# A four-part sequence network with 32 experts: blocks shared ten to six between the two sets of expert tiles, and three gathers in flight beside the tiles

## What is computed

```python
x = x + _L0_attn_ref(_layernorm(x), ...)        # delta rule
x = x + _L0_ffn_ref(_layernorm(x), ...)         # 8 of 32 experts a token, plus a shared one
x = x + _L1_attn_ref(_layernorm(x), ...)        # h = dA_t * h + dBx_t, then y = hs @ C.T + D * x
x = x + _L1_ffn_ref(_layernorm(x), ...)         # quantized in blocks of 32, then @ weight.T
```

## Time and profile before

| | |
|---|---|
| median of 3 runs | 3666.69 us (3666.28 to 3671.66) |
| the profiled execution | 3663.13 us |
| its span | 3661.3 us |
| PE, DVE, ACT, POOL busy | 74%, 59%, 43%, 29% of the span |
| chain that ended last | DMA 55% (scatters 40%, gathers 14%), PE 28%, issue 7%, DVE 5% |
| granted TensorE clock, mean | 0.825 |

### The profile page before, as it was taken

The page is one execution under the profiler, slowest core; times in us unless marked ns, Lnnn a source line. Parts: engine busy times, 40 slices in busy tenths (PEclk is TensorE's granted clock), DMA queues, the critical chain, the costliest instruction groups (busy, mean ns, idle before and its releaser), DMA issues.

```text
span 3661.3 us, 109753 instructions
## 1 busy us (share of the span) xinstructions
PE 2712.2 (74%) x46188; PEld 2021.3 (55%) x46188; DVE 2153.5 (59%) x4702; ACT 1565.2 (43%) x2625; POOL 1048.7 (29%) x1028
## 2 busy tenths in 40 slices
PE   4578888888878887875207999997898888643544
PEld 2355555555555655554106888886777777422322
DVE  4878888888888888772201222213444444676675
ACT  4445555545544555511003444444555554432231
POOL 0001333333332333333330000014434431366661
PEclk8768788888888788766558999998999999876666
DMA  6001111111114111111317999997888887333331
GB/s 241 8 9 36 61 56 61 50 64 62 62 62 148 62 61 55 56 56 57 141 52 245 303 305 304 304 311 232 266 280 262 272 266 247 120 94 94 99 93 34
DMA packets 240349, 511.79 MB, mean 140 GB/s; under 512 B 38770, under 2 KB 63860, under 8 KB 239732
## 3 DMA queue, kind: packets, MB, share of 16 engines
q1 hardware_dynamic: 133396, 270.32, 22.6%
q0 software_dynamic: 49152, 134.28, 11.8%
q10 hardware_dynamic: 57312, 100.16, 7.5%
HBM read 303.82 MB, written 200.80 MB: 138 GB/s over the span
## 4 chain that ended last, share of the span: by engine, by line
DMA 55%; PE 28%; issue 7%; DVE 5%; ACT 3%; POOL 1%; SPq 0%; ACTq 0%; POOLq 0%; DVEq 0%
DMA scr_xs<-xn_r,idx 40%; DMA yg<-scr_ys,idx_y 14%; PE ps L629 13%; PE ps L637 6%; PE ps L618 3%; DVE tmp L1426 1%; DVE tu L1429 1%; PE ps L377 1%; DVE conv L1356 1%; PE ps L706 1%; PE ps L669 1%; DMA out<-x 1%; POOL yg L869 1%; PE ps L688 1%; PE ps L364 0%
## 5 line engine op out<-in xcount | busy, mean ns | idle before, releaser
L851 POOL DMA_INDIRECT scr_xs<-xn_r,idx x512 | 528.9, 1033 | 1407.5 <-DMA scr_xs<-xn_r,idx 1062.4
L869 POOL DMA_INDIRECT yg<-scr_ys,idx_y x512 | 519.7, 1015 | 1129.2 <-DMA scr_ys<-y 574.4
L1721 DVE TENSOR_TENSOR h<-sg,ps 128x256 f32<-128x256 f32 x318 | 133.1, 420 | 829.3 <-ACT sg L1106 790.6
L629 PE MATMUL ps<-xT,wr 128*128 128x256 f32 x2544 | 617.1, 386 | 0.0
L629 PEld LDWEIGHTS ps<-xT,wr 128*128 128x128 f32 x2544 | 470.5, 195 | 62.0 <-issue 8.6
L1748 DVE SCALAR_TENSOR_TENSOR x<-yg,wsel,x 128x256 f32<-128x256 f32 x512 | 247.8, 485 | 220.3 <-DMA yg<-scr_ys,idx_y 201.9
L637 PE MATMUL ps<-wr,h 128*128 128x256 f32 x1272 | 334.1, 386 | 57.8 <-DVE h L1721 31.5
L914 ACT ACTIVATE xT<-ps 128x512 f32<-128x512 f32 x382 | 225.3, 594 | 210.5 <-PE ps L618 173.2
L618 PE MATMUL ps<-identity,xt 128*128 128x128 f32 x1272 | 195.7, 277 | 149.9 <-DMA xt<-scr_xs 149.9
L637 PEld LDWEIGHTS ps<-wr,h 128*128 128x128 f32 x1272 | 242.9, 192 | 98.4 <-DVE h L1721 34.0
L914 ACT ACTIVATE y<-ps 128x512 f32<-128x512 f32 x318 | 189.8, 597 | 202.0 <-PE ps L637 186.8
(11 more groups left out here) (244 smaller groups left out, 4216.8 us busy)
## 6 DMA issues: line engine op xcount, KB each, us to landing
wr<-in_wexp SPq DMA_DIRECT2D x318, 384.0 KB
xt<-scr_xs SPq DMA_DIRECT2D x318, 256.0 KB
scr_ys<-y ACTq DMA_DIRECT2D x318, 256.0 KB
scr_xs<-zeros SPq DMA_DIRECT2D x128, 256.0 KB
x_in<-in_x SPq DMA_DIRECT2D x64, 128.0 KB
x_res<-in_x SPq DMA_DIRECT2D x64, 128.0 KB
scr_xs<-xn_r,idx POOLq DMA_INDIRECT x512, 2.6
scr_x<-x_res SPq DMA_DIRECT2D x16, 512.0 KB
```

The lines of the kernel that those rows point to most:

```text
L629: last = pe.matmul(ps[:, bank, half * TILE:(half + 1) * TILE], wr[:, t % NW, at:at + EI], xT2[:, t % NH, k, :], start=k == 0, stop=k == G - 1)
L851: nc.gpsimd.indirect_dma_start(xs[i // HB][:, :], bass.IndirectOffsetOnAxis(idx[:, i % 2, c, k:k + 1], 0), xn_r[:, i % 2, c, :], None).the ...
L869: nc.gpsimd.indirect_dma_start(yg[:, n % NG, k, :], None, ys[h][:, :], bass.IndirectOffsetOnAxis(idx_y[:, i, c, k:k + 1], 0))\
```

## The change

Blocks 0 to 9 belong to the first set of tiles and blocks 10 to 15 to the second. CAP becomes 4 * 10 * 128 + 256 = 5376 rows (4352 before). The sets have NTH = [191, 127] tiles; NT stays 318. The tiles that run alone are 191. SL = 13, and a helper `Share` hands out 13 slots in an iteration at the places where 22 were handed out, each in proportion. `slots(NT)` and the iterations without tiles begin at i == 8 and no longer at 6. `tables(0)` runs behind block 9 and `clear_ends(0)` in step 11, both two steps later. The gathers count on four semaphores in place of two, for each of which `combine` waits. For blocks 0 to 9 a gather waits for the third before it, for blocks 10 to 15 for the second as before.

```diff
+class Share:
+    def __init__(self, run, per, of):
+        self.run, self.per, self.of, self.at, self.done = run, per, of, 0, 0
+    def __call__(self, weight):
+        self.at += weight
+        want = self.at * self.per // self.of
+        self.run(want - self.done)
+        self.done = want
...
-    if "P" in on and (on["P"] + 1) % (NB // 2) == 0:
-        on["H"] = on["P"] // (NB // 2)
+    if "P" in on and on["P"] + 1 in (NB * 5 // 8, NB):
+        on["H"] = int(on["P"] + 1 == NB)
...
-    CAP = B * T // HALVES + TILE
-    NTH = B * T // HALVES * TOPK // TILE + E - 1
-    NT = HALVES * NTH
-    NQ = -(-NTH // P)
+    FIRST = (NB * 5 // 8, NB)
+    CAP = B * FIRST[0] * TB + TILE
+    NTH = [B * TB * blocks * TOPK // TILE + E - 1 for blocks in (FIRST[0], NB - FIRST[0])]
+    NT = sum(NTH)
+    NQ = -(-max(NTH) // P)
...
-        SL = -(-(NTH + LAG - 30) // (HB - 2))
+        SL = -(-(NTH[1] + LAG - 30) // (FIRST[0] - 2))
...
-        s_yg = [sem(f"s_yg{n}") for n in range(2)]
+        s_yg = [sem(f"s_yg{n}") for n in range(4)]
...
-                if i == HB - 2:
+                if i == FIRST[0] - 2:
                     slots(NT)
                     banks = tuple(range(8))
                 if i:
                     quant_turns(i - 1)
                 skips(i)
-                slots(2)
+                share(2)
                 outputs(i)
-                slots(1)
+                share(1)
                 if i:
                     quant_rows(i - 1, 0)
-                slots(2)
+                share(2)
                 if i:
                     quant_rows(i - 1, 1)
-                slots(5)
+                share(5)
                 if i + 1 < NB:
                     delta_turns(i + 1)
-                    slots(2)
+                    share(2)
                     deltas(i + 1)
-                    slots(1)
+                    share(1)
                     inputs(i + 1)
-                    slots(2)
+                    share(2)
                     means(i + 1)
-                slots(SL - 15)
+                share(7)
...
-                if j == HB + 1:
+                if j == FIRST[0] + 1:
                     clear_ends(0)
...
-                        if fetched >= 2:
-                            pool.wait_ge(s_yg[fetched % 2], 16 * (fetched // 2))
+                        landed = fetched - (3 if i < FIRST[0] else 2)
+                        if landed >= 0:
+                            pool.wait_ge(s_yg[landed % 4], 16 * (landed // 4 + 1))
...
-                for way in range(2):
-                    dve.wait_ge(s_yg[way], 16 * TOPK // 2 * (n + 1))
+                for way in range(4):
+                    dve.wait_ge(s_yg[way], 16 * TOPK // 4 * (n + 1))
```

More of the change, by code:

```diff
@@ L656, in _ @@
             turn_tile(1)
-            slots(NTH)
+            slots(NTH[0])
             def delta_turns(i):
@@ L729, in outputs @@
                     done(last, bank)
+            share = Share(slots, SL, 22)
             slots(23)
@@ L857, in _ @@
             for i in range(NB):
-                h = i // HB
-                if i % HB == 0:
+                h = int(i >= FIRST[0])
+                if i in (0, FIRST[0]):
                     for n in range(NY):
-                        pool.wait_ge(s_ys[n], 16 * (-(-(NTH * (h + 1) - n) // NY)))
+                        pool.wait_ge(s_ys[n], 16 * (-(-(sum(NTH[:h + 1]) - n) // NY)))
                 for c in range(NC):
@@ L1207, in _ @@
                     quant_turns(i - 1)
-                slots(6)
+                share(6)
                 root("quant", i)
@@ L1211, in _ @@
                     root("tail", i + 1)
-                slots(2)
+                share(2)
                 if i + 1 < NB:
                     tail_rows(i + 1)
-                slots(2)
+                share(2)
                 if i + 1 < NB:
                     delta_turns(i + 1)
-                    slots(2)
+                    share(2)
                     softplus(i + 1)
-                    slots(3)
+                    share(3)
                     decays(i + 1)
-                slots(SL - 15)
+                share(7)
                 if i:
@@ L1734, in _ @@
                 rows_of_y(p)
[L1735 to L1736 removed]
+                slots(NTH[0] // NB)
+            slots(NTH[0] % NB)
             def combine(i, c, k0=0, k1=TOPK):
                 n = NC * i + c
[L1740 to L1741 removed]
+                for way in range(4):
+                    dve.wait_ge(s_yg[way], 16 * TOPK // 4 * (n + 1))
                 if c == 0 and k0 == 0:
@@ L1753, in combine, with combine_between @@
                     last.then_inc(s_comb, 1)
-            def combine_between(i, c):
+            def combine_between(i, c, run=slots):
                 combine(i, c, 0, TOPK // 2)
-                slots(1)
+                run(1)
                 combine(i, c, TOPK // 2)
-                slots(1)
+                run(1)
             def tail_means(i):
@@ L1794, in quant_rows @@
                 sQ.did(normalize(xq, x3[:, i % NX3], "quant", i, sQ))
-                slots(1)
+                share(1)
                 sQ.wait(dve)
-                quantize(xq[:].rearrange("p c d -> p (c d)"), qb[:], qc[:], NC * D // QB, sQ, slots)\
+                quantize(xq[:].rearrange("p c d -> p (c d)"), qb[:], qc[:], NC * D // QB, sQ, share)\
                     .then_inc(s_xn["quant"], 1)
+            share = Share(slots, SL, 22)
             slots(9)
```

41 lines of the change are left out of this document (19 added, 22 removed).

## The result

The changed kernel takes 3759.0 us (3719.0 to 3784.3, 4 runs) and the kernel before, on the same chip, 3669.2: a ratio of **1.021 [1.013, 1.029]**. Ratios here compare means, and an execution over 1.5% above the fastest of its kernel, such as the one at 3784.3, is left out of them. The forecast was 3614, with 3655 as its upper end; the direction is wrong. The span of the profiled execution is 3761.2, 99.9 us more than before.

A forecast was written before the change was run, and what follows sets the result against it. The prediction took scatters, then PE on tiles, then gathers (tail, 55.1 us a block) as limits. 2533.7 + 147 + 66.0 + 6 x 74.0 + 12.8 + 328.9 + 76.5 = 3608.9, plus 5.4: 3614 us, range 3585 to 3655.

The forecast's parts named there:

- The third gather: Start of the shared stretch: with three in flight, gathers come every 1.8 us in place of 2.41.
- the lead-in: From the start of the shared stretch to `deltas(1)`: 147 us, 36.9 less than before.
- The tail: Second set's gathers: 192 in place of 256 at 1.722 us, 110 us less, then 76.5 as before.
- Iterations with tiles: Shared stretch: 13 slots in place of 22 take 27.2 us out of each; 66.0, then six of 74.0.
- cover term: Iterations with tiles: fewer slots between hand-overs add 2.0 us each, between 0 and 6.3, taken from PE's idle time.
- The first whole iteration: `deltas(1)` to `deltas(2)`, without the wait for `out`: 64.0 us plus 2.0 added, so 66.0.
- the third gather without effect: Rival, shared stretch: DMA sets 2.41 us a gather, 320 gathers in a row, 3724 us; chance 0.07.
- thin cover: Rival, iterations with tiles: hand-overs show in full, 6.3 us added and not 2.0, 3644 us; chance 0.13.
- PE idle over 17 us in an iteration: Sign in iterations with tiles that the forecast is wrong through cover; 13 us of idle time was forecast.
- CAP, tables, semaphores: Edits put at nothing: addresses change, two steps move; two more waits per combination, 0.5 us a block on DVE with slack.
- The 8 us allowed for the scatters: Before the first tile: scatters go one at a time as before, 8 us allowed either way.
- The locked port: Rival, gathers' issue: each as long as the longest, 1.97 us, a rate of 2.27, 3679 us; chance 0.02.

The follow-up runs named there:

- e2: Kernel before (eight to eight) with three gathers in flight for the first set only, chip 1: 0.990 of the kernel before.
- e1: Changed kernel with two gathers in flight throughout (ten to six), chip 1: 1.006 of the kernel before.
- a2: Changed kernel run again as it is, chip 5, no stops: 0.993 of the kernel before.
- e10: Changed kernel (ten to six) with three gathers in flight for all blocks, chip 15: 0.972 of the kernel before.
- e8: Kernel before (eight to eight) with three gathers in flight for all blocks, chip 5: 0.965 of the kernel before.
- a3: Changed kernel run again as it is, chip 15, no stops: 0.991 of the kernel before.
- a4: Changed kernel run again as it is, chip 7, with stops: 1.023 of the kernel before.
- e4: Kernel before with only the changed kernel's larger CAP, chip 1: 1.000 of the kernel before.
- e6: Kernel before (eight to eight) with four gathers in flight for the first set, chip 5: 0.988 of the kernel before.
- e1c: Changed kernel with two gathers in flight throughout (ten to six), chip 7, no stops: 1.005 of the kernel before.
- e8b: Kernel before (eight to eight) with three gathers in flight for all blocks, chip 7, with stops: 1.016 of the kernel before.

## Why the prediction was wrong

- **The third gather** did what was forecast: 1.76 us against 1.8. By itself it is worth 1203.8 - 1174.8 = 29 us of stretch (e2), at a ratio of 0.990; the forecast had 36.9 in the lead-in. Beside the ten-to-six division it is worth more, 1327.2 - 1283.6 = 43.6 us, as the iteration from `deltas(1)` to `(2)` too waits for gathers when two are in flight (80.6 us in e1, 65.6 in a2).
- **The tail** did as well: 406.2 against 405.4, 110 less.
- **The failed step is "Iterations with tiles"**, twice. First, its cover term was mis-sized. Where no stop disturbs, the six iterations average 78.5 us (79.8 to 76.9 in a2), not 74.0. In the one shown 6.4 us are added to the 72.0, just above the upper end of 6.3 that the prediction drew: 13.7 - 11.2 = 2.5 of idle time, most of it the wait for DVE's addition, and 3.9 of busy time. The prediction took PE's busy time as given and asked only after its idle time; the waits between fewer tiles put the clock at its lower level three times in an iteration, once before. The first whole iteration, at 65.6 in a2 against 66.0, shows that the rest of the working held, as does the idle time of 13.7 us against the 13.2 forecast (11.2 and 2.0).
- On a chip without stops the forecast is thus off by 1283.6 - 1261.6 = 22 us of stretch (its own sum gives 3203.5 - 1941.9). The changed kernel gains 0.7 to 0.9% there, against the 1.4% forecast, and 3667 and 3680 us lie above the range, since the kernel before is itself some 30 us longer on those chips.
- **The ten-to-six division gains nothing.** It costs 0.4 to 0.6% with two in flight (e1), 0.7% with three throughout (e10 against e8), and about nothing with three for the first set alone. With two in flight, two blocks more make the stretch 1327.2 - 1203.8 = 123 longer and the tail 106 to 110 shorter; with three, 1283.6 - 1174.8 = 109 longer and 105 to 109 shorter. What a block costs beside tiles, 109 / 2 = 54.5, is what it costs in the tail, 55.1. The gain in a2 and a3 is that of the third gather alone.
- Second, and this gave the direction: **the stops**, of which "Iterations with tiles" has no term. In the recorded profile and in a4 they hold 150 and 111 us of ACT's time, and the stretch is 100 to 107 longer than on chips without them. No rival had them. The rival that came nearest in time, the third gather without effect (3724), names a rate of 2.41 that wasn't there, and the sign named for thin cover, PE idle over 17 us in an iteration, would have misled: it is 124.9 / 6 = 20.8 in the recorded profile and 13.7 where nothing stops. The rival that was missing is that with a third gather in flight other engines stand still while POOL issues. Nothing in the trace of before shows it, where two are in flight and POOL waits for a landing before 355 of its 512 gathers.
- **CAP, tables, semaphores** cost nothing, as said (e4, and 1283.4 to 1283.7 twice). The 8 us allowed for the scatters were too few: first tiles of one and the same program lie 28 us apart (1957.7 to 1985.6). So were the 7 us named as what a measurement of this kernel can tell: the four executions of the changed kernel alone lie 65 us apart.
- The locked port played no part: a gather's issue is 1004 ns on average after, 1015 before. The Trainium skill's rule, page "SBUF — State Buffer", section "SBUF: two separate sides", costs nothing that these rows show, with three in flight either.

Open are: what begins a stop, what it stops (the trace can't tell the delivery of instructions from a semaphore that doesn't arrive), whether spacing the gathers prevents it, and why some chips have none. e2, e6 and e10 weren't run on chip 7, so their ratios hold for the other chips alone, as does the 0.965 of e8.

## What to carry to other kernels

Work moved from one stretch to another pays only by the difference of its price in the two: cost a block in both, here 54.5 and 55 us, before counting what the emptied stretch saves. Where a wait for landings paces a queue, loosening it by one can gain much (0.965 on one chip) and can lose on another (1.016); look for waits whose releaser is unknown, and time such a kernel on several chips before it is kept. With less work between hand-overs, price a wait at itself and what the lower clock behind it adds.

## What the runs showed of the hardware

**Chips differ, and a stretch with no gathers in it tells the kinds apart.** In 0 to 1900 us every kernel here runs the same 38860 matmuls. Windows of that stretch of e1c (chip 7) and of a2 (chip 5), and from each the group of 8192 of the small matmuls:

```profile
0.00:1900.00 1900.00, 1349.26 (x38860) 921.48 (x38860) 1379.55 (x3140) 820.23 (x1233) 516.76 (x499) 0.79 0.21 70
L420 PE MATMUL ps<-r_sb,tt 32*32 32x16 f32 x8192 | 150.0, 206 | 54.3 <-issue 33.0
```

```profile
0.00:1900.00 1900.00, 1279.44 (x38860) 889.79 (x38860) 1378.41 (x3140) 820.29 (x1233) 505.99 (x486) 0.79 0.20 69
L420 PE MATMUL ps<-r_sb,tt 32*32 32x16 f32 x8192 | 135.5, 206 | 54.5 <-DVE r_sb L1459 34.2
```

PE's busy time is 1349 to 1361 us in the six traces from the recorded chip and chip 7, and 1274 to 1295 in the fourteen from chips 1, 5, 9, 14 and 15, at about the same granted clock (0.78 to 0.79, and 0.78 to 0.80); DVE and ACT agree to 0.3%. A matmul doesn't take longer: the mean of these 8192 is 206 or 207 ns in all twenty traces. But they overlap less, and PE is busy with them for 147.7 to 151.6 us in the six and for 134.8 to 135.9 in the fourteen. All four traces with stops are among the six (the other two have two gathers in flight). So the kind of chip can be read before the gathers begin. Small matmuls that follow one another more slowly, and a stop in which PE does one in 2.8 us with nothing to wait for, could have one cause in how instructions reach the engine; that isn't shown. With the recorded chip not named, the first kind may be one chip or two.

**In a stop the instruction streams of PE, ACT and DVE go slow together while POOL's doesn't**: one matmul in 2.8 us, no ACT instruction for 57 us, DMA engines 64% idle (e8b); 12 matmuls and no DVE instruction in 35 us of a4, where a2 has 202 and 45.
